# A two-stage Trainium2 kernel: the transposes of the second half's x2 tiles move from TensorE to DMA

## The reference, cut to what matters

```
x  = x + layernorm(attn(layernorm(x)))     # attn: circular convolution, decaying causal sum over
                                           # tokens, circular correlation, gate, plus its input
x2 = layernorm(x)
gate, up = x2 @ w_gate.T, x2 @ w_up.T      # w: int32 / 127, 1024 -> 3072
out = x + layernorm((silu(gate) * up) @ w_down.T)   # 3072 -> 1024
```

## Time and profile before

| | us |
|---|---|
| median of 3 runs | 579.08 (578.75 to 579.83) |
| the profiled execution's own time | 579.18 |
| its span on the slowest core, 7 | 576.8 |
| spans of the other cores | 575.2 to 576.5 |
| PE busy | 558.6 (97% of the span) |
| DVE, POOL, ACT busy | 322.0, 262.9, 181.4 |

### The profile page before, as it was taken

One profiled execution on the slowest core, in us unless ns is written; L12 is line 12 of the kernel. 1 busy time (PEld: TensorE's weight loads), 2 busy tenths in 40 slices (PEclk: granted clock), 3 DMA queues, 4 the chain that ended last, 5 costly groups with the idle time before them and its releaser, 6 DMA issues.

```text
span 576.8 us, 8369 instructions; the slowest of 8 cores (575.2 to 576.8 us)
## 1 busy us (share of the span) xinstructions
PE 558.6 (97%) x2708; PEld 255.7 (44%) x2708; DVE 322.0 (56%) x507; ACT 181.4 (31%) x251; POOL 262.9 (46%) x432
## 2 busy tenths in 40 slices
PE   8789999999999999999999999999999999999994
PEld 3444444444444444444444444444444444444442
DVE  3887747676546511113243268898998987223222
ACT  3566751144223521122332323233333232001011
POOL 2677773356314511000111679989999970001010
PEclk9999999999999999999999999999999999999998
DMA  7972119666728398400026914444655400000101
GB/s 209 339 158 49 28 28 145 102 98 105 104 44 129 64 157 124 76 0 37 36 59 129 179 74 68 79 73 74 100 92 98 76 1 2 36 37 36 74 37 73
DMA packets 14203, 49.51 MB, mean 86 GB/s; under 512 B 1744, under 2 KB 3152, under 8 KB 13392
## 3 DMA queue, kind: packets, MB, share of 16 engines
q0 software_dynamic: 8544, 31.46, 34.5%
q1 hardware_dynamic: 5328, 17.45, 8.6%
q10 hardware_dynamic: 288, 0.07, 0.1%
HBM read 72.04 MB, written 8.39 MB: 139 GB/s over the span
## 4 chain that ended last, share of the span: by engine, by line
PE 88%; DVE 4%; issue 3%; DMA 2%; POOL 2%; ACT 1%; DVEq 0%; POOLq 0%; ACTq 0%; SPq 0%
PE pb L524 14%; PE pa L524 13%; PE pc L711 11%; PE pa L711 11%; PE pa L804 7%; PE pb L711 7%; PE pc L804 7%; PE pb L804 7%; PE psc L804 4%; PE pc L382 2%; DMA x<-xin 2%; PE pc L308 1%; PE pt L474 1%; DVE sta L248 1%; PE pc L372 1%
## 5 line engine op out<-in xcount | busy, mean ns | idle before, releaser
L253 POOL TENSOR_SCALAR r<-mv 128x1 f32<-128x1 f32 x32 | 6.7, 209 | 185.5 <-DVE mv L724 167.9
L524 PE MATMUL pa<-x2t,wgu 128*128 128x512 f16 x384 | 87.6, 379 | 0.9 <-ACT sil L532 0.8
L524 PE MATMUL pb<-x2t,wgu 128*128 128x512 f16 x384 | 87.8, 379 | 0.0
L711 PE MATMUL pa<-wd,h 128*128 128x512 f16 x276 | 61.5, 379 | 0.0
L711 PE MATMUL pc<-wd,h 128*128 128x512 f16 x276 | 61.5, 379 | 0.0
L524 PEld LDWEIGHTS pa<-x2t,wgu 128*128 128x128 f16 x384 | 37.0, 98 | 44.7 <-issue 1.8
L524 PEld LDWEIGHTS pb<-x2t,wgu 128*128 128x128 f16 x384 | 37.1, 98 | 42.8
L732 DVE SCALAR_TENSOR_TENSOR x<-v,gf,x 128x1024 f32<-128x1024 f32 (+1 forms) x17 | 21.6, 1278 | 39.7 <-ACT v L730 39.7
L258 POOL TENSOR_TENSOR r<-r,nhf 128x1 f32<-128x1 f32 x64 | 36.9, 576 | 9.5
L711 PE MATMUL pb<-wd,h 128*128 128x512 f16 x184 | 41.0, 379 | 0.0
L711 PEld LDWEIGHTS pa<-wd,h 128*128 128x128 f16 x276 | 26.9, 98 | 31.9
(11 more groups left out here) (187 smaller groups left out, 907.8 us busy)
## 6 DMA issues: line engine op xcount, KB each, us to landing
wgu<-wgu POOLq DMA_DIRECT2D x24, 512.0 KB, 7.2
wp<-wgu POOLq DMA_DIRECT2D x22, 512.0 KB, 8.9
x<-xin SPq DMA_DIRECT2D x16, 512.0 KB, 8.0
out<-x SPq DMA_DIRECT2D x15, 512.0 KB, 2.6
wd<-wdt POOLq DMA_DIRECT2D x6, 1024.0 KB, 14.2
wph<-wgu POOLq DMA_DIRECT2D x2, 512.0 KB, 10.3
out<-x SPq DMA_DIRECT2D x2, 256.0 KB, 2.1
hkf<-hki SPq DMA_DIRECT2D x1, 394.5 KB, 7.6
```

The source lines that it names most:

```text
L524: tok = P.put("tensor", lambda e_, d=d: e_.matmul(ten[:, 512 * half:512 * half + 512], WGU[s][:, 1024 * half + 128 * d:1024 * half + 128 * ...
L711: tok = P.put("tensor", lambda e_, fc=fc, e=e: e_.matmul(pair[:, 512 * fc:512 * fc + 512], (H, HB)[hf][e][:, 128 * tl:128 * tl + 128], WD[ ...
```

## The change

In `down(0, tl)` the 8 PE transposes and the ACT copy are gone. In their place `x2t_dma` issues 8 DMAs from SP's queue, each with `transpose=True`, from a 128 by 128 block of x2s right into its place in X2T. They wait for x2 of the tile and for `dn_start`, and share one semaphore `tr`; x2t[t] and evt[t], which `x2_op` of the next tile and `token_sums` wait for, are now the landing of the eighth. The first half (tiles 0 to 7) keeps its PE transposes.

```
-    def dma(self, eng, out, in_, name, *toks):
+    def dma(self, eng, out, in_, name, *toks, **how):
...
+    def x2t_dma(t, *toks):
+
+        for d in range(ND):
+            evt[t] = x2t[t] = P.dma("sync", X2T[:, 1024 * d + 128 * (t % 8):1024 * d + 128 * (t % 8) + 128],
+                                    X2S[:, 128 * d:128 * d + 128], "tr", x2[t], *toks, transpose=True)
...
             if hf == 0 and fc == 0:
-                x2t_mm(ORD2[tl])
-                evt_op(ORD2[tl], "scalar", dn_start)
+                x2t_dma(ORD2[tl], dn_start)
                 if tl % 2 == 1:
                     token_sums(tl // 2)
```

More of the change, by code:

```diff
@@ L67, in dma @@
         self.val[name] += 16
-        self.q[eng].append(lambda e, o=out, i=in_, s=self.sem[name]: e.dma_start(out=o, in_=i).then_inc(s, 16))
+        self.q[eng].append(lambda e, o=out, i=in_, s=self.sem[name]: e.dma_start(out=o, in_=i, **how).then_inc(s, 16))
         return (name, self.val[name])
```

## The result

| | us |
|---|---|
| before, median of 4 runs | 579.37 (578.75 to 579.83) |
| changed, median of 4 runs | 628.53 (626.47 to 629.65) |
| ratio | 1.085, 95% interval 1.0834 to 1.0866 |
| profiled execution, changed | 629.65, its slowest core (4) spans 628.0 |

A forecast was written before the change was run, and what follows sets the result against it. PE was taken to bound the kernel, with the last token sums only 1.0 us before PE needs them. Later sums 2.9, weight loads 10.3 and restart 1.6 made +14.8 us, so 594.0 us; range 580 to 655.

The forecast's parts named there:

- T: End of DVE's last token sum, 338.15 us before the change; forecast 341.0, moving everything after it by 2.9 us.
- The links: Steps from one transpose group's landing to the next first issue: 7.7 us after odd tiles, 1.3 after even ones.
- odd link: After an odd tile's landing: token sums, statistics, scaling, copies and store before the next first issue, 7.7 us.
- The price i: Time of one transposing block on SP's queue: 0.53 us, taken from the load of the identity.
- The first rival: Blocks pass one at a time on the queue at 1.17 us each, giving 620 to 630 us; chance 0.33.
- B = 8i + 2.1: Time from a group's first issue on SP to its last landing, eight blocks plus a store's landing: 6.3 us.
- +46 us: Side calculation: the skill's 1309 ns per block on the queue would put T at about 385, 46 us later.
- The loads: Weight loads beside the transposes of tiles 10, 14 and 11 delay their landings: 10.3 us, bounds 0 and 20.7.
- The restart: PE starting again after standing at the second block of `pair(0)` for some 15 us: 1.6 us added.
- PSUM: PE's down tiles are not stopped earlier: three pairs exist, and L730 would have to be over 20 us late.
- Page against row: Skill pages disagreed on transposing DMAs: as fast as regular ones, or 1309 ns per block; no profile row decided.

The follow-up runs named there:

- experiment 10: experiment 4's kernel with the three weight loads and first weight sums moved behind the last down tile; 599.84 us in its one run, a time not used.
- experiment 11: The changed kernel with weight loads and first weight sums moved behind the last down tile; only T read, 380.3 us on core 4, 377.9 on core 7.
- experiment 2: The kernel before without any transposes or copies of tiles 8 to 15; 575.06 us, ratio 0.993.
- experiment 5: The changed kernel with a second x2s buffer and one semaphore per buffer; 620.25 us, ratio 1.0707.
- experiment 6: The changed kernel with an odd tile's token sums moved on DVE from ahead of its statistics to behind its L737; 610.18 us, ratio 1.0539.
- experiment 1: The changed kernel with its 64 DMAs copying plainly instead of transposing; 598.48 us, ratio 1.0336.
- experiment 3: The changed kernel with each transposing DMA split into two of 64 tokens by 128 features, 16 per tile; 700.96 us, ratio 1.21.
- experiment 12: The changed kernel with its transposing DMAs issued from ACT's queue instead of SP's; 625.25 us, ratio 1.0788.
- experiment 4: The changed kernel with one transposing DMA for a whole tile, 128 by 1024, in place of eight; 591.47 us, ratio 1.021.
- experiment 9: experiment 8's kernel with the token sums of tiles 10 and 14 moved on DVE ahead of tile 6's statistics; 577.47 us, ratio 0.9962.
- experiment 8: Against the kernel before: seven tiles transposed by one DMA each, the last on PE, two x2s buffers, token sums a tile later on DVE; 577.73 us, ratio 0.9971.

## Why the prediction was wrong

1. *What bounds the kernel, and T.* Right. In both kernels, and in every run but 10 and 11 (where PE waits for the moved loads), the profiled cores 4 and 7 have 238.7 to 240.4 us from T to the end, while T goes from 333.5 (experiment 2) to 460.0. One thing was missing: PE first stands at the first block of `pair(0)`, 30.6 us, because at this price tile 11's x2 lands only at 373.3. The forecast had PE stand at the second block alone.
2. *The links.* Right: 7.7 and 1.3 forecast, 7.9 and 1.4 measured, and experiments 5 and 6 took 8 and 18 us out of them. Only the odd link after tile 14 was longer, 9.7 us, with L737 at 3.1 us beside POOL's weight sums.
3. *The price i.* This is the step that failed: "I take 0.53", the nearest row, a plain load's issue. Measured: 0.62 for a plain block (experiment 1), 1.24 to 1.27 for a transposing one. It stands on the chain 7 x 7 times. The first rival, i = 1.17 and 620 to 630 us, was the case that came; it had 0.33. That its numbers fit so well is partly luck: 1.17 is only the middle, by ratio, of two far bounds, and its sum carries the error of point 4.
4. *B = 8i + 2.1.* The landing counts from the last block's issue, so the eighth i was counted twice. It is 7 x 1.27 + 2.37 = 11.3. From core 4's first chained issue at 270.1: 270.1 + 7 x 11.3 + 29.1 (the links and last sums) = 378.3 us; without loads 380.3 were measured, the rest being long issues (a group's 10.9 and 11.1 in place of 10.1). With the forecast's own B and the right i the sum would have been 7 us too long. The two errors had opposite signs, and i's was by far the larger. So the +46 us that the forecast worked out beside it for i = 1.309 us, and that core 7's T then showed, is luck too: with this B it would have been about 39, without loads.
5. *The loads.* 10.3 us taken. That landings beside the loads are late was right, but of the three groups named only one was hit hard: tile 10's landed 6.84 us after its last issue (332.53) on core 4 and 8.44 on core 7 in place of 2.3, so 4.5 and 6.1 us; the later loads fell beside groups that were still being issued. With plain blocks (experiment 1) all three were hit, by 9 us together, near the forecast.
6. *The restart.* 1.6 us taken, at most 0.6 measured (240.0 against 239.4 us behind T). PE stood for 30.6 and then 12.9 us, and the granted clock is at half in these stretches of core 4 (the columns are stretch, length, busy times and counts of PE, PEld, DVE, ACT, POOL, clock, DMA share, GB/s):

```profile
348.00:373.00 25.00, 0.00 (x0) 0.00 (x0) 8.89 (x12) 3.35 (x3) 12.94 (x16) 0.50 0.46 78
373.00:388.00 15.00, 1.86 (x4) 0.43 (x4) 1.73 (x5) 1.24 (x1) 0.64 (x1) 0.50 0.17 53
388.00:395.00 7.00, 6.67 (x20) 2.54 (x21) 3.74 (x6) 2.20 (x3) 4.87 (x6) 0.63 0.12 50
```

   A clock of 0.50 is 1.2 GHz. Of PE's blocks behind T (start, us, four matmuls each) the first three take nearly twice as long as the next:

```profile
388.33 1.86 PE L809 MATMUL pb<-wgu,ws 128*128 128x512 f16 x4 [12.92 <-DVE wgu L753]
...
393.33 1.03 PE L809 MATMUL pc<-wgu,ws 128*128 128x512 f16 x4
```

   They ran while the statistics of tile 7 had to be waited for anyway, so what they cost was hidden. The half clock after standing still is what the Trainium skill states, "TensorE: Matmul & The Clock Gate", section "What's actually happening"; the rows above agree with it.
7. *PSUM.* "PSUM does not stop PE earlier" was wrong at i = 1.27: PE waited 3.8 us in stage 2 for L735. It cost nothing, T being later still.
8. *Page against row.* The Trainium skill, "VectorE: DVE Perf Modes", The three transpose paths, gives 1309 ns for such a block by DMA; the 1.24 to 1.27 us from issue to issue come within 3 to 5% of it, and in a row too, which I had doubted. (From its issue to its landing a single block took 2.3 to 2.4 us.) The Trainium skill, "Advanced Engine Details and Errata", X-Bar Transpose (TRN2), has transposing DMAs as fast as regular ones. Per DMA that fails here by a factor of two (1.27 against 0.62 us). A whole tile in one DMA, 256 KB, landed in 3.8 us, where a plain store of as many bytes took 2.1; no run has the plain copy of the same shape.

The account of core 7's +46.0 us in T: the chain of groups and links at the normal issue, from its first issue at 266.7 with B = 7 x 1.24 + 2.37 = 11.05, ends at 373.2, so 35 us. Tile 10's landing adds 6.1, L737 beside the weight sums 1.8, and issues longer than normal 2.4. That leaves under 1 us, which the links' 7.9 and 1.4 in place of 7.7 and 1.3 explain. Why single issues take up to 2.5 us in the changed kernel is open.

## What to carry to other kernels

Count the instructions on a DMA queue before the bytes: a transposing DMA of 64 by 128 and one of 128 by 128 both cost 1.23 us of issue, and one of 128 by 1024 cost 1.47. Use one DMA per tile, buffer its source twice, and let nothing in an in-order list wait for it that others need. And where a trace does not show an operation and its bounds lie a factor of five apart, the nearest row is one case, not the likely one: here it was out by a factor of 2.4, 49 times over.

## What the runs showed of the hardware that I had not expected

- The issue of a transposing DMA holds SP's queue for 1.20 us on odd cores and 1.23 us on even ones (medians), for half a block too (experiment 3), and ACT's for 1.23 and 1.27 (experiment 12). Plain SBUF to SBUF blocks of the same size hold it for 0.59 us, a 512 KB store for 0.33.
- A transposing DMA of a whole tile lands in 3.0 to 5.5 us away from the loads on POOL's queue and in 6.7 to 15.1 beside them (experiments 4, 9 and 10, all cores), though it holds only 256 KB; two buffers and a tile of slack hide the first, and the second only in part (experiments 8 and 9).
- The best version, experiment 9, gains 0.38% (0.24 to 0.52%), 2.2 us and about half of what removing the transposes altogether gives (4.1 us); experiment 8's 0.29% can't be told from it.
